# Transposing the normalised rows of attention: block transposes of VectorE and sixteen DMAs in place of TensorE's products

## The reference

```python
def xcond(x, latents, shift, scale, ...):           # x: ctx (16, 128, 256), latents: layernorm of x
    x   = layer_norm(x, ln1_w, ln1_b)
    lat = layer_norm(latents, ln2_w, ln2_b)
    lat = lat * (1 + scale[:, None, :]) + shift[:, None, :]
    q   = lat @ Wq.T                                # 16 heads of 64
    k, v = split(concatenate((x, lat), axis=-2) @ Wkv.T)
    w   = softmax(q k^T / 8)
    return (w v) @ Wo.T
x = x + xcond(ctx, layernorm(x), cond, cond, ...)
x = x + ffn(layernorm(x), ...)                      # shared expert and top 1 of 8 experts
```

## Time and profile before

| | |
|---|---|
| time, median of 3 runs | 709.05 us (708.55 to 709.14) |
| profiled execution | 707.77 us, its span 706.0 us |
| TensorE busy | 689.7 us (98%) |
| VectorE busy | 474.6 us (67%) |
| ScalarE busy | 439.8 us (62%) |
| GpSimd busy | 255.9 us (36%) |
| attention | about the first 430 us of the span |

### The profile page before, as it was taken

How to read it: one execution, slowest core, us unless ns; L and a number is a source line. 1 busy time by engine, 2 the same in 40 slices (tenths; PEclk the granted TensorE clock), 3 DMA queues, 4 the chain that set the end, 5 groups by cost and what they waited for, 6 DMA issues and landing times. The chain is left out here.

```text
span 706.0 us, 18044 instructions
## 1 busy us (share of the span) xinstructions
PE 689.7 (98%) x6037; PEld 640.1 (91%) x6038; DVE 474.6 (67%) x993; ACT 439.8 (62%) x1208; POOL 255.9 (36%) x406
## 2 busy tenths in 40 slices
PE   7899999999999999999999999999999899999997
PEld 7789999899899998999989978898889899999997
DVE  5878888887877878888888675366545655333343
ACT  4787887887878878788787875242344544223232
POOL 4924223232332321422546541057131344423333
PEclk9999999999999999999999999999999999999999
DMA  8343444444444343444445433004557976767660
GB/s 296 95 124 96 123 112 115 117 107 115 112 125 109 98 134 106 108 124 104 117 118 137 116 81 127 1 0 117 163 204 267 326 284 231 274 234 273 224 256 12
DMA packets 54473, 103.80 MB, mean 147 GB/s; under 512 B 12700, under 2 KB 32926, under 8 KB 51744
## 3 DMA queue, kind: packets, MB, share of 16 engines
q1 hardware_dynamic: 44336, 85.80, 39.4%
q0 software_dynamic: 7072, 14.71, 7.5%
q10 hardware_dynamic: 3024, 2.76, 1.3%
HBM read 59.81 MB, written 12.74 MB: 103 GB/s over the span
## 5 line engine op out<-in xcount | busy, mean ns | idle before, releaser
L915 PE MATMUL PS<-BIG 128*128 128x256 f32 (+1 forms) x1164 | 196.0, 322 | 0.6 <-issue 0.4
L915 PEld LDWEIGHTS PS<-BIG 128*128 128x128 f32 x1164 | 166.1, 189 | 14.8 <-issue 1.0
L1908 PE MATMUL PS<-XST,W 128*128 128x128 f32 x1012 | 118.4, 277 | 1.9 <-issue 1.9
L582 ACT ACTIVATE PR<-PS,NMX 128x256 f32<-128x256 f32 x256 | 117.8, 475 | 2.9 <-DVE NMX L740 2.8
L1908 PEld LDWEIGHTS PS<-XST,W 128*128 128x128 f32 x1012 | 116.5, 194 | 2.2 <-issue 2.1
L591 ACT ACTIVATE PR<-PR,RINV 128x256 f32<-128x256 f32 x256 | 105.9, 517 | 0.4 <-DVE RINV L747 0.4
L752 DVE STREAM_TRANSPOSE PR<-PR 128x512 f32<-128x512 f32 x124 | 80.6, 687 | 2.5 <-ACT PR L591 2.0
L437 POOL DMA_DIRECT2D PT<-PR x128 | 64.6, 510 | 44.0 <-DVE PR L752 37.3
L740 DVE TENSOR_REDUCE NMX<-PS 128x4 f32<-128x1024 f32 x64 | 75.4, 1197 | 1.8 <-PE PS L973 1.8
L935 PE MATMUL PS<-KVF,WQ 128*128 128x128 f32 x512 | 65.6, 281 | 1.6 <-DVE BIG L728 1.1
L935 PEld LDWEIGHTS PS<-KVF,WQ 128*128 128x128 f32 x512 | 59.6, 192 | 7.0 <-issue 5.0
(11 more groups left out here) (190 smaller groups left out, 1192.7 us busy)
## 6 DMA issues: line engine op xcount, KB each, us to landing
W<-in_w SPq DMA_DIRECT2D x21, 1408.0 KB, 5.9
PT<-PR SPq DMA_DIRECT2D x368, 64.0 KB, 2.0
PT<-PR POOLq DMA_DIRECT2D x128, 64.0 KB, 2.4
W<-in_w SPq DMA_DIRECT2D x8, 640.0 KB, 4.0
xs_sorted<-ZERO SPq DMA_DIRECT2D x26, 128.5 KB, 3.1
W<-in_w SPq DMA_DIRECT2D x8, 352.0 KB, 3.4
XS<-xs_sorted ACTq DMA_DIRECT2D x21, 128.5 KB, 2.8
RC<-in_ctx SPq DMA_DIRECT2D x16, 128.0 KB, 2.7
```

Source lines behind the costliest of these rows:

```text
L582: last = act.activation(probs, logits, ACT.Exp, bias=NMX[:, g, own, p % 2:p % 2 + 1], accum_out=SUM[:, p, own:own + 1])
L915: last = pe.matmul(dst, stat(s, k), mov(m, k), start=n == 0, stop=n == len(todo) - 1)
L1908: last = pe.matmul(h[:, P * c:P * (c + 1)], lhs13(W13[par], k, c), XST[par][:, k, :], start=k == 0, stop=k == KD - 1)
```

## The change

The normalised rows of batches 1 to 15 are no longer transposed by TensorE. `CN` and `XN` become the halves of one tile `CXN`. VectorE transposes its blocks of 32x32 in place, in one call of 128x512, at the end of half (b, 1) for batch b + 2 (batch 1: in half (0, 0)). SP then moves the blocks to their quadrants with sixteen DMAs into `INT`, each 32 partitions by two runs of 64 elements, after its moves of probabilities of half (b, 1). `modulate` reads `INT` in SBUF in place of the bank in PSUM, and waits for the sixteen DMAs instead of for TensorE. It stays where it was in VectorE's list. The order in which the features land on the partitions is another one (blocks of 32 are interleaved), so the host permutes the features of the weights, norms and conditions, and gives batch 0's rows a second, permuted copy; batch 0 itself is still transposed by TensorE. To make room, the zero rows take the place of the last batch's rows in `C`, so the last `expert_input` waits for the stores of them.

```diff
@@ SP
+            def move_inputs(n):
+                sp.wait_ge(v_cxn, n)
+                if not isinstance(n, int) or n > 1:
+                    sp.wait_ge(v_kvf, n)
+                for i in range(4):
+                    for j in range(4):
+                        sp.dma_start(INT[QUADS[j], i, :, :], CXN[QUADS[i], :, 64 * j:64 * (j + 1)]).then_inc(d_int, 16)
+
             def batch(n, rows=True, first=False, last=False):
                 if rows:
                     load_rows(n + 2)
+                if first:
+                    move_inputs(1)
                 move_probs(n, 0)
                 load_residual(n)
                 if not first:
                     store_sum(n - 1)
                 if not last:
                     move_probs(n, 1)
+                if rows:
+                    move_inputs(n + 2)
@@ VectorE
-            def norm_rows(n, guard=True):
+            def norm_rows(n):
                 dve.wait_ge(p_rs, n + 1)
-                if guard:
-                    dve.wait_ge(t_in, n)
...
+            def transpose_inputs(n):
+                dve.wait_ge(v_xn, n + 1)
+                dve.transpose(CXN[:, :, :], CXN[:, :, :]).then_inc(v_cxn, 1)
+
             def modulate(n, par):
 
-                dve.wait_ge(t_in, n + 1)
                 dve.wait_ge(v_aff, n + 1)
+                dve.wait_ge(d_int, 16 * 16 * n)
                 if not isinstance(n, int) or n > 1:
                     dve.wait_ge(p_kvl, n - 1)
+                keys = KVF[par][:, :, :].rearrange("p k (t i q) -> p k t i q", t=2, i=4)
                 for k in range(KD):
-                    src = PS[:, OB, KEYS * k:KEYS * (k + 1)]
-                    if not (isinstance(n, int) and n == 0):
-                        modulate_ctx(k, par)
-                    last = dve.tensor_scalar(KVF[par][:, k, P:KEYS], src[:, P:KEYS], AFF[:, 0, k:k + 1],
+                    part = slice(32 * k, 32 * (k + 1))
+                    dve.tensor_scalar(keys[:, k, 0, :, :], INT[:, :, 0, part], LNP[:, 0, k:k + 1], LNP[:, 1, k:k + 1],
+                                      ALU.mult, ALU.add)
+                    last = dve.tensor_scalar(keys[:, k, 1, :, :], INT[:, :, 1, part], AFF[:, 0, k:k + 1],
                                              AFF[:, 1, k:k + 1], ALU.mult, ALU.add)
                 last.then_inc(v_kvf, 1)
@@ VectorE, half
                     row_max(h, 1)
                     if first:
                         norm_again(1)
+                        transpose_inputs(1)
...
                 if not final:
                     for p in (2, 3):
                         transpose_blocks(h, H, p)
+                if H == 1 and norm:
+                    transpose_inputs(b + 2)
@@ VectorE, end of attention
+            dve.wait_ge(d_zero, 16 * 2 * (NB - 3))
             expert_input(NB - 1)
@@ TensorE
-            def transpose_inputs(n):
-
-                pe.wait_ge(v_xn, n + 1)
-                if not isinstance(n, int) or n > 1:
-                    pe.wait_ge(v_ol, 2 * (n - 1) - 1)
-                for k in range(KD):
-                    for i, src in enumerate((CN, XN)):
-                        last = pe.transpose(PS[:, OB, KEYS * k + P * i:KEYS * k + P * (i + 1)],
-                                            src[:, 128 * k:128 * (k + 1)], IDENT[:, :])
-                last.then_inc(t_in, 1)
-
@@ TensorE, times_v
-                if H == 1:
-                    pe.wait_ge(v_kvf, b + 3 if not isinstance(b, int) else min(b + 3, NB))
@@ TensorE, half
-                    if H == 0 and not last:
-                        transpose_inputs(b + 1)
```

More of the change, by code:

```diff
@@ L158, in attention_part @@
         AFF = sb("AFF", [128, 2, KD])
-        CN = sb("CN", [128, D])
-        XN = sb("XN", [128, D])
+        CXN = sb("CXN", [128, 2, D])
+        CN, XN = CXN[:, 0, :], CXN[:, 1, :]
+        INT = sb("INT", [128, 4, 2, 2 * 32])
         ST = sb("ST", [128, 4, 6])
@@ L171, in attention_part @@
         X2 = sb("X2", [128, D])
-        ZERO = sb("ZERO", [128, DI])
+        ZERO = C[:, NB - 1, :]
         KVF = [sb(f"KVF{i}", [128, KD, KEYS]) for i in range(2)]
@@ L239, in attention_part @@
         v_xn = sem("v_xn")
+        v_cxn = sem("v_cxn")
+        d_int = sem("d_int")
         v_st2 = sem("v_st2")
@@ L310, in load_rows @@
                     sp.wait_ge(v_xn1, n)
-                sp.dma_start(RC[:, :], one(a["ctx"], n)).then_inc(d_rows, 16)
-                sp.dma_start(RX[:, :], one(a["x"], n)).then_inc(d_rows, 16)
+                ctx_n, x_n = (a["first"][i] if isinstance(n, int) and n == 0 else one(a[name], n)
+                              for i, name in enumerate(("ctx", "x")))
+                sp.dma_start(RC[:, :], ctx_n).then_inc(d_rows, 16)
+                sp.dma_start(RX[:, :], x_n).then_inc(d_rows, 16)
             def load_residual(n):
@@ L373, in _ @@
                 for t in (2 * n - 2, 2 * n - 1):
-                    sp.dma_start(mem["xs"][bass.ds(t * P, P), :], ZERO[:, :]).then_inc(d_zero, 16)
+                    sp.dma_start(mem["xs"][bass.ds(t * P, P), :], ZERO).then_inc(d_zero, 16)
             sp.wait_ge(p_wsl, FT)
@@ L401, in _ @@
             pool.memset(MHALF[:, :], -0.5).then_inc(p_const, 1)
-            pool.memset(ZERO[:, 0:D], 0.0).then_inc(p_const, 1)
-            pool.memset(ZERO[:, D:DI], NOBODY).then_inc(p_const, 1)
+            pool.memset(C[:, NB - 1, 0:D], 0.0).then_inc(p_const, 1)
+            pool.memset(C[:, NB - 1, D:DI], NOBODY).then_inc(p_const, 1)
             pool.memset(EPST[:, :], EPS).then_inc(p_const, 1)
@@ L859, in _ @@
             dve.wait_ge(v_cond, 4)
-            norm_rows(0, guard=False)
+            norm_rows(0)
             dve.wait_ge(t_cn0, 1)
             for k in range(KD):
-                last = modulate_ctx(k, 0)
+                last = modulate_first(k, 0)
             last.then_inc(v_ctx0, 1)
             norm_again(0)
-            modulate(0, 0)
+            dve.wait_ge(t_in, 1)
+            dve.wait_ge(v_aff, 1)
+            for k in range(KD):
+                last = modulate_first(k, 1)
+            last.then_inc(v_kvf, 1)
             keys_lo(dve, 0, 0, v_wk_lo)
@@ L1071, in transpose_first @@
                 for k in range(KD):
-                    last = pe.transpose(PS[:, OB, KEYS * k + P * i:KEYS * k + P * (i + 1)], src[:, 128 * k:128 * (k + 1)],
-                                        IDENT[:, :])
+                    last = pe.transpose(PS[:, OB, KEYS * k + P * i:KEYS * k + P * (i + 1)],
+                                        src[:, 128 * k:128 * (k + 1)], IDENT[:, :])
                 return last
@@ L1984 @@
     ws2, ws2_last = hidden_rows(L0_ffn_ws2_FD)
+    features = np.arange(D).reshape(4, KD, 32).transpose(1, 0, 2).reshape(D)
     norms = np.stack([np.asarray(v) for v in (L0_xcond_ln1_w, L0_xcond_ln1_b, L0_xcond_ln2_w, L0_xcond_ln2_b)])
     given = {
-        "x": x, "ctx": ctx_1024, "cond": np.moveaxis(on_partitions(cond_1024), 1, 2), "ln": on_partitions(norms),
-        "wq_t": np.asarray(L0_xcond_Wq).T, "wkv_t": np.asarray(L0_xcond_Wkv).T, "wo_t": np.asarray(L0_xcond_Wo).T,
+        "x": x, "ctx": ctx_1024, "first": np.stack([np.asarray(ctx_1024)[0], np.asarray(x)[0]])[:, :, features], "cond": np.moveaxis(on_partitions(np.asarray(cond_1024)[:, features]), 1, 2),
+        "ln": on_partitions(norms[:, features]),
+        "wq_t": np.asarray(L0_xcond_Wq).T[features], "wkv_t": np.asarray(L0_xcond_Wkv).T[features], "wo_t": np.asarray(L0_xcond_Wo).T,
         "router": L0_ffn_router_DE, "w13": hidden_columns(L0_ffn_w1_eDF, L0_ffn_w3_eDF), "w2": w2, "w2_last": w2_last,
```

16 lines of the change are left out of this document (9 added, 7 removed).

## The result

The changed kernel takes 844.19 us (median of 4 runs, 842.12 to 844.63) against 709.1; the ratio is 1.189, with an interval of 1.187 to 1.192. The forecast was 833, with a range of 780 to 880. The profiled execution took 844.02 us for a span of 842.2, so 136.2 us have to be found in the span.

What follows compares the result with a forecast made beforehand. TensorE was taken to set the pace, 25.45 us a batch; waiting for SP's sixteen moves would make it 33.6. Span 706.0 + 8.7 for batch 0 + 115 for 14 periods, + 1.8 + 1.3 = 833 us; range 780 to 880.

Steps and rivals of the forecast that it cites:

- S to the modulation: From S, the start of SP's twelve second-half moves of probabilities, until the next batch's modulation can begin: 19.0 us.
- the sixteen issues: SP's new moves of inputs, issued behind its twelve: 0.625 us each, 9.4 us to the last issue.
- The modulation and the transposes: On VectorE after the wait: the modulation 1.2 us, then three transposes of probabilities 1.8 us.
- VectorE's second half: From the first half's last transposes to SP's next second-half moves: 12.9 us today, 11.6 with waits for ScalarE gone.
- TensorE's clock: Idle some 8 us a batch, TensorE drops to 1.2 GHz; loss taken as 0, without cover 24 us more.
- TensorE's gain: Four input transposes fewer in each of 15 batches, 0.45 us a batch: at most 6.7 us.
- The sum: Fourteen periods of attention, each 8.2 us longer at 33.6 against 25.4 us: 115 us added to the span.
- Batch 0: Its modulation begins 9.2 us late, 0.5 of it regained in the second half's waits: 8.7 us added.
- Cheap issues: Rival: SP's moves go at 0.45 us each, as row loads do, period 31.0: 793 us; chance 0.10.
- dear ones: Rival: SP's issues take 0.8 us and more, 887 us at 0.87, or TensorE's cold clock comes through, 857; chance 0.13 over 880.
- The queue alone: Rival: SP's own work binds at 28.9 us a batch, VectorE's wait not carrying over: 767 us; chance 0.03.
- Faster: Rival: the sixteen moves fit in and TensorE's 0.45 us a batch come back: 702 us; chance 0.01.

Runs made afterwards that it cites:

- Experiments 1 to 4: The changed kernel with no moves of inputs (705.16 us), four (715.93 us), eight (755.45 us), and all sixteen with a quarter of the bytes (842.32 us).
- experiment 7: The changed kernel with the modulation behind all four block transposes of the first half instead of behind the first: 843.41 us.
- experiment 10: The changed kernel with 28 products of the identity ahead of TensorE's wait for the modulation, in batches 2 to 15: 834.5 us.
- Experiment 1: The changed kernel without the moves of inputs, VectorE's block transpose writing straight to `INT`: 705.16 us, ratio 0.995.
- experiment 11: The kernel before with eight more GpSimd transfers, read by nobody, in each of batches 1 to 15: 706.7 us against 705.67, ratio 1.0015.
- experiment 8: The changed kernel with twelve moves on GpSimd, four on SP, modulation behind all four transposes, V copied before keys are rounded, batch 1 transposed by TensorE: 721.39 us.
- experiments 6 and 8: The first is the changed kernel with GpSimd issuing the sixteen moves from batch 2 on: 754.64 us; the second is experiment 8.
- experiments 5 and 10: The changed kernel with products of the identity ahead of TensorE's wait for the modulation, in batches 2 to 15: 64 of them 913.0 us, 28 of them 834.5 us.

## Why the prediction was right, and where its terms were off

*What decides.* Right in mechanism and place: the modulation waits for the sixteen moves, SP issues them behind twelve others, and the loop closes through VectorE's order. S to the modulation was forecast 19.0 and measured 19.07; the sixteen issues 9.4 to the last one's start, measured 9.6 (0.64 each); landing 2.0, measured 1.8. Experiments 1 to 4 confirm it: without the moves nothing is lost, each move adds 0.64 us to the modulation's start, and bytes do not count.

*The modulation and the transposes.* 1.02 and 1.81 against 1.2 and 1.8.

*VectorE's second half.* The largest miss of a term: forecast 11.6 us, measured 12.18 (312.50 to 324.68). The reason given for it, "VectorE is then busy through this half, so this is its floor", does not hold in the changed kernel: experiment 7 took the same 14.0 us from the modulation to S without the three transposes in between. It holds only at full clock, where the half is 11.29 (experiment 10, 309.62 to 320.91). So 11.6 was 0.3 too long for its own reason and left out the 0.88 of the clock; that these partly cancel, some 4 us of the whole, is luck.

*TensorE's clock.* "I take 0" was wrong. The clock fell as forecast and the queries' products lost 1.7 us, as forecast; but not all of it was hidden. 0.88 us a batch comes through, 9.3 us over experiment 10's fourteen periods, where the bound without cover allowed 24. The cover that the prediction counted on is there, but it is 0.8 us long (13.11 against 12.35), not 1.7.

*TensorE's gain.* At most 6.7 us was right as a bound: without the moves, 0.34 us a batch. The Trainium skill (TensorE: Matmul & The Clock Gate, PE-mode transpose) gives 390 ns for a 128x128 bf16 transpose in isolation; an estimate by that figure would have been 23 us. Experiment 1 decides for the distance between starts.

*The sum.* 115 was 124.6. Of the 0.70 us a batch that were missed, 0.6 are the second half, less 0.2 for the shorter modulation, and 0.1 comes ahead of the modulation; the last 0.2 are early and late batches: the sixteen took 11.36 and 10.99 us in the first two batches and 11.54 in the last, and periods there are 34.7 and 35.5. Batch 0 had 9.3 for 8.7: its modulation began at 37.00 and not 36.5, 9.7 late, and 0.4 of that was regained.

*The experts.* Forecast as before, and 2.2 us longer. The same stretch was 274.0 to 275.9 us in the ten experiments that hold the change in some form, and 273.5 and 271.3 in the two kernels without it (before, and experiment 11), which also differ from each other by 2.2 with the same code there. The cause was not found, and differences of this size between traces taken on different occasions show none.

*The rivals.* Cheap issues (0.45 us) and dear ones (0.87) are both excluded by 240 issues at a median of 0.597 us, 0.64 from start to start. The queue alone (767 us) is excluded by the wait of 9.48 us on VectorE. Faster is what experiment 1 shows when the price is taken away.

No version here does the whole work and beats the kernel before. The nearest is experiment 8, 1.7% slower; its steady batches are 0.15 us shorter, which in fourteen batches would be worth 2 us at best. The Trainium skill (VectorE: DVE Perf Modes, "The three transpose paths") says that VectorE's transpose works on blocks of 32x32 only. Its "Rules for kernel authors" name TensorE for a 128x128 transpose where PSUM will do as the destination. The runs agree: the blocks cost 0.6 us and nothing on the path, and bringing them to their quadrants 10.25 us of a queue.

## What to carry to other kernels

Cost a transfer that is cut into pieces by its number of issues on the queue, behind what that queue already holds: here sixteen small moves were 10 us, at 16 KB as at 4 KB, while the four products that they replaced were 0.3 to 0.45 together. Before you call a slower stage hidden, follow both chains from the same event to the same event: VectorE's list looked full, and half of TensorE's slow clock came through a second chain only 0.8 us shorter. An engine's gap that costs nothing where its result has slack (experiment 11) can cost twice its length where it has none (experiment 8).

## What the runs showed of the hardware beyond that

- GpSimd's issuing of transfers stops for 2.7 to 2.9 us after its first 128, in three kernels with different transfers at different times (191.2, 198.6 and 233.8 us). It stops a second time for 2.6 to 3.0 us, after 120 more in experiments 6 and 8 and after 116 more in experiment 11; what sets that number is open. The kernel before issues exactly 128 of these in attention, so no move of its own stands behind such a stop.
- An issue on SP with 32 partitions costs 0.63 to 0.64 us from start to start, whether it moves 4, 16 or 64 KB and whether it reads SBUF or DRAM; the loads of rows from DRAM into 128 partitions are 0.45 apart. On GpSimd issues with 32 partitions are 0.50 to 0.56 apart.
- Behind a store of 256 KB (128 pieces of 2 KB) on SP the next nine issues took 0.82 us each instead of 0.63.
- A matmul of two f32 tiles of 128x128 left two records of 0.11 us each on TensorE in experiments 5 and 10, while a transpose of the same size left one.
